# A factorization machine on one core: V's loads go first on two queues, and GpSimd holds back x until two thirds of V have landed

## The reference

```python
def reference(x, V, bias, g_bias):          # x: int32 512 x 6250, V: fp32 6250 x 64
    xf = x.astype(V.dtype)
    xv = xf @ V
    sum_sq = jnp.sum(xv * xv, axis=-1)
    sq_sum = xf @ jnp.sum(V * V, axis=-1)
    linear = g_bias + xf @ bias
    return linear + (0.5 * (sum_sq - sq_sum))[:, None]
```

## Time and profile before

| | us |
|---|---|
| median of 3 runs | 48.98 (48.85 to 49.02) |
| profiled execution | 49.03 |
| its span | 47.2 |
| busy: DVE | 30.5 (65%) |
| busy: PE | 22.0 (46%) |
| busy: POOL | 20.5 (43%) |
| busy: ACT | 13.7 (29%) |

### The profile page before, as it was taken

How to read it: one execution, slowest core, us unless ns; L and a number is a source line. 1 busy time by engine, 2 the same in 40 slices (tenths; PEclk the granted TensorE clock), 3 DMA queues, 4 the chain that set the end, 5 groups by cost and what they waited for, 6 DMA issues and landing times.

```text
span 47.2 us, 634 instructions
## 1 busy us (share of the span) xinstructions
PE 22.0 (46%) x210; PEld 20.1 (43%) x210; DVE 30.5 (65%) x74; ACT 13.7 (29%) x30; POOL 20.5 (43%) x34
## 2 busy tenths in 40 slices
PE   0000000000000000045999995999999999997200
PEld 0000000000000000045989893998999899985100
DVE  2000000000999469997999899999999999998600
ACT  0000009100899469954996300020002000000000
POOL 1999800000199009999599999990000000000000
PEclk9999999999999999999999999999999999999998
DMA  0399999999999999999999999999999970000000
GB/s 0 102 152 100 109 140 152 164 189 158 175 174 172 181 170 178 146 142 108 105 106 106 106 106 106 101 104 103 116 96 101 94 55 3 0 0 0 0 2 0
DMA packets 5583, 4.87 MB, mean 103 GB/s; under 512 B 1434, under 2 KB 5581, under 8 KB 5581
## 3 DMA queue, kind: packets, MB, share of 16 engines
q0 software_dynamic: 3456, 3.21, 73.4%
q1 hardware_dynamic: 1155, 0.82, 6.7%
q10 hardware_dynamic: 970, 0.81, 5.3%
HBM read 14.48 MB, written 0.00 MB: 307 GB/s over the span
## 4 chain that ended last, share of the span: by engine, by line
DVE 42%; DMA 34%; ACTq 10%; issue 4%; PE 2%; ACT 1%
DMA v_in<-in_L_rec_V_dram 34%; DVE x_all L330 13%; DVE seen L344 13%; ACTq L150 5%; DVE v_rest L295 3%; ACTq L237 3%; DVE xv L354 3%; DVE w_sum L301 2%; DVE xv_sq L359 2%; DVE odd_turned L335 2%; PE xv_ps L466 2%; ACTq L233 2%; DVE seen L406 1%; ACTq L234 1%; DVE seen L350 1%
## 5 line engine op out<-in xcount | busy, mean ns | idle before, releaser
L466 PE MATMUL xv_ps<-wall,x_all 128*128 128x195 bf16 x192 | 19.9, 266 | 1.8 <-DVE x_all L330 1.8
L466 PEld LDWEIGHTS xv_ps<-wall,x_all 128*128 128x128 fp8e4 x192 | 18.0, 105 | 2.7 <-DVE x_all L330 1.1
L160 POOL DMA_DIRECT2D x_all<-in_r_x_dram x24 | 13.0, 551 | 0.8 <-POOLq L498 0.8
L216 POOL TENSOR_TENSOR wall<-v_rest 128x512 bf16<-128x512 f32 (+1 forms) x6 | 7.4, 1247 | 10.2 <-DVE v_rest L295 10.2
L450 PE MATMUL g_ps<-g_in,ones 1*128 1x1 f32 x2 | 0.6, 342 | 20.2 <-DMA g_in<-in_L_rec_g_bias_dram 20.2
L450 PEld LDWEIGHTS g_ps<-g_in,ones 1*128 1x128 f32 x2 | 0.5, 305 | 20.2 <-issue 20.2
L330 DVE STREAM_TRANSPOSE x_all<-x_all 128x512 uint32<-128x512 uint32 (+1 forms) x13 | 8.5, 652 | 0.0
L364 DVE MEMSET v_in<- 22x64 f32 x1 | 0.1, 112 | 10.6 <-DMA v_in<-in_L_rec_V_dram 10.6
L344 DVE TENSOR_TENSOR seen<-seen,x_all 128x512 uint32<-128x512 uint32 (+1 forms) x10 | 6.3, 628 | 0.0
L251 ACT ACTIVATE v_sq<-v_in 128x512 f32<-128x512 f32 (+1 forms) x6 | 3.8, 636 | 5.3 <-DVE v_in L364 3.5
L295 DVE TENSOR_TENSOR v_rest<-v_in 128x512 f32<-128x512 f32 (+1 forms) x6 | 4.3, 750 | 1.4 <-DMA v_in<-in_L_rec_V_dram 1.3
(11 more groups left out here) (27 smaller groups left out, 9.5 us busy)
## 6 DMA issues: line engine op xcount, KB each, us to landing
x_all<-in_r_x_dram POOLq DMA_DIRECT2D x12, 196.0 KB, 9.7
v_in<-in_L_rec_V_dram ACTq DMA_DIRECT2D x6, 128.0 KB, 13.3
v_in<-in_L_rec_V_dram SPq DMA_DIRECT2D x6, 128.0 KB, 11.3
x_all<-in_r_x_dram POOLq DMA_DIRECT2D x4, 100.0 KB, 7.4
x_all<-in_r_x_dram POOLq DMA_DIRECT2D x4, 64.0 KB, 8.5
x_all<-in_r_x_dram POOLq DMA_DIRECT2D x4, 32.0 KB, 8.1
bias_in<-in_L_rec_bias_dram ACTq DMA_DIRECT2D x3, 6.5 KB
v_in<-in_L_rec_V_dram SPq DMA_DIRECT2D x1, 24.0 KB
```

The costliest lines, as they stand in the source:

```text
L160: queue.dma_start(x_words[S * i:S * i + S, t, :, lo // QUAD:hi // QUAD].bitcast(fp8), rows[:, :, START[i] + lo:START[i] + hi]).then_inc(x_ ...
L216: nc.gpsimd.tensor_tensor(placed(n, 2), v_part(v_rest, n), upper(v_rest, n), ALU.subtract).then_inc(low_placed, 1)
L466: last = nc.tensor.matmul(xv_ps[t][:, :, :], rows[:, q, :], wall[:, 1 + QUAD * d + q, :, 0:E], start=(d + q == 0), stop=(d == ND - 1 and q ...
```

## The change

POOL gets one wait ahead of its first x issue: `v_landed[1]` must be full, that is, V's second load must have landed in all four quarters. SP issues nothing but V's quarters 0 and 1 first; the odd rows of V go to ACT, behind its two DMAs of load 0; the five bias DMAs and g go behind V on SP. On DVE the two `sum_squares` of load 0 move ahead of the wait for the bias.

```diff
@@ block.sync
-            first = S * (NQ - 1)
-            sp.dma_start(v_in[0:first, 0, :],
-                         V[0:Q * (NQ - 1), :].rearrange("(i l) f -> i l f", l=Q)[:, 0:S, :]).then_inc(v_landed[0], 16)
-            sp.dma_start(v_in[first:P, 0, :], V[START[NQ - 1]:START[NQ - 1] + S, :]).then_inc(v_landed[0], 16)
             for n in range(NL):
                 load_v(sp, n, (0, 1))
+            sp.wait_ge(bias_cleared, 1)
+            sp.dma_start(bias_in[0:1, W - S:W], bias[0:S, :].rearrange("l o -> o l")).then_inc(bias_landed, 16)
...
+            sp.dma_start(g_in[:, :], g_bias.rearrange("(a b) -> a b", b=1)).then_inc(g_landed, 16)
@@ block.gpsimd
+            pool.wait_ge(v_landed[1], V_COUNT[1])
             load_x(pool, 0)
             load_x(pool, 1)
@@ block.scalar
+            first = S * (NQ - 1)
             load_v(act, 0, (2, 3))
-            act.wait_ge(bias_cleared, 1)
-            act.dma_start(bias_in[0:1, W - S:W], bias[0:S, :].rearrange("l o -> o l")).then_inc(bias_landed, 16)
...
+            act.dma_start(v_in[0:first, 0, :],
+                          V[0:Q * (NQ - 1), :].rearrange("(i l) f -> i l f", l=Q)[:, 0:S, :]).then_inc(v_landed[0], 16)
+            act.dma_start(v_in[first:P, 0, :], V[START[NQ - 1]:START[NQ - 1] + S, :]).then_inc(v_landed[0], 16)
             load_v(act, 1, (2, 3))
             load_v(act, 2, (2, 3))
-            act.dma_start(g_in[:, :], g_bias.rearrange("(a b) -> a b", b=1)).then_inc(g_landed, 16)
@@ block.vector
             keep_rest(0)
             keep_rest(1)
+            sum_squares(0)
+            sum_squares(1)
             dve.wait_ge(bias_landed, 16 * (NQ + 1))
...
-            sum_squares(0)
-            sum_squares(1)
             weigh(0)
```

More of the change, by code:

```diff
@@ L188, in _ @@
         def _(sp):
-            first = S * (NQ - 1)
-            sp.dma_start(v_in[0:first, 0, :],
-                         V[0:Q * (NQ - 1), :].rearrange("(i l) f -> i l f", l=Q)[:, 0:S, :]).then_inc(v_landed[0], 16)
-            sp.dma_start(v_in[first:P, 0, :], V[START[NQ - 1]:START[NQ - 1] + S, :]).then_inc(v_landed[0], 16)
             for n in range(NL):
                 load_v(sp, n, (0, 1))
+            sp.wait_ge(bias_cleared, 1)
+            sp.dma_start(bias_in[0:1, W - S:W], bias[0:S, :].rearrange("l o -> o l")).then_inc(bias_landed, 16)
+            sp.dma_start(bias_in[1:1 + ND, :], bias[S:Q, :].rearrange("(d l) o -> d (l o)", l=W)
+                         ).then_inc(bias_landed, 16)
+            for i in range(1, NQ):
+                sp.dma_start(bias_in[S * i:S * i + 1 + ND, :],
+                             bias[START[i] + S - W:START[i] + Q, :].rearrange("(d l) o -> d (l o)", l=W)
+                             ).then_inc(bias_landed, 16)
+            sp.dma_start(g_in[:, :], g_bias.rearrange("(a b) -> a b", b=1)).then_inc(g_landed, 16)
             y_out = out.rearrange("(p m) o -> p (m o)", m=T)
```

## The result

The changed kernel takes 54.11 us (53.41 to 55.03, 4 runs) against 49.0 us before: ratio 1.0992, 95% interval 1.0877 to 1.1107. It is 5 us slower where I had forecast 1.4 us faster. The profiled execution took 54.12 us with a span of 52.2.

What follows compares the result with a forecast made beforehand. The prediction took DVE's list and x's DMA stream, side by side, as the bound. DVE's slack of 0.54 us at tile 3 plus x landing 0.85 us earlier gave 1.4: 49.03 - 1.4 = 47.6 us, range 47.0 to 49.4.

Steps and rivals of the forecast that it cites:

- What bounds the kernel: DVE's work and x's DMA run side by side; DVE is only 1.25 and 0.54 us behind tiles 2 and 3.
- How fast V goes alone: V's loads on both queues without x: bounds 196 and 332 GB/s, 300 taken.
- When x starts: POOL's x loads after the wait: v_landed[1] full at 5.6 us, x's data flowing from 7.1 instead of 2.8.
- The gap is near nothing: DMA engines between V and x: V's last third ends at 7.1 us, when x's data begin to flow.
- When x lands: x's pieces 0 to 2 need 22.9 us at 105 GB/s; tile 2 lands at 30.3, 0.85 us earlier.
- The comparison: On the DMA engines: V costs x about 5.5 us when mixed in, 4.7 when put ahead.
- The bias: SP's bias loads behind V land at 9.5 us; DVE waits one microsecond, hidden by the wait for piece 0.
- POOL: POOL's eight x issues after the wait take 4.42 us, to 10.0; later pieces are issued without starvation.
- The sum: Whole kernel: 49.03 - 1.4 = 47.6 us, from 0.54 us of slack at tile 3 and x landing 0.85 earlier.
- Rival 1: V alone runs at the one-queue 196 GB/s: x flows from 9.0, end 1.1 us later at 50.1; chance 0.20.
- Rival 2: TensorE falls to its slow pace waiting for tile 2: 1.2 of 2.2 us count, 48.8 us; chance 0.12.

Runs made afterwards that it cites:

- e7: Kernel before with one 2048-column memset on POOL ahead of its first x issue; 48.93 us, ratio 0.9932 to the kernel before.
- e5: Changed kernel with V's odd rows behind all of ACT's V loads, POOL's wait kept; 51.24 us, ratio 1.0434 to the kernel before.
- e3: Changed kernel with POOL's wait on v_landed[0] in place of v_landed[1]; 52.81 us, ratio 1.0755 to the kernel before.
- e6: Changed kernel without POOL's wait and with V's odd rows back at the head of SP's queue; 57.4 us, ratio 1.1666 to the kernel before.
- e4: Changed kernel with 36 extra matmuls, read by nothing, behind tile 1's last one in TensorE's pause; ratio 1.0716 to the kernel before.
- e8: Kernel before with only V's odd rows moved from SP's head to ACT behind its load 0; 55.35 us, ratio 1.1174 to the kernel before.
- e2: Changed kernel without POOL's wait, the new queue order kept; 53.5 us, ratio 1.0851 to the kernel before.
- e1: Kernel before with only POOL's wait on v_landed[1] added, queues in their old order; 53.38 us, ratio 1.0756 to the kernel before.

## Why the prediction was wrong, point by point

- *What bounds the kernel* was read rightly. The slack of 1.25 us at tile 2 is what the short delays use up; in e7 DVE waits 2.12 us for tile 2 and loses nothing by it.
- *How fast V goes alone*: the step "Two queues at 196 each would be 392, so the engines cap them ... I take 300" held for V's own pieces: 292 GB/s, in the changed kernel for two microseconds and in e5 for all five. It failed for what stands between them. I had looked at the odd rows on SP as something that no longer stands in front, and not at the 128 pieces of 256 bytes that now stand in ACT's queue between its first loads and its second. With them the rate falls to 221 GB/s at a share of 0.99, and x's first issue comes at 10.19 instead of 7.11. The row of 196 GB/s was also read too simply: SP had issued the first 24 KB of odd rows by 1.7 us, so some of them may have been moving in it.
- *When x starts*: the step "5.3, and I add 0.3 ... 5.6" was mis-sized by 4.6 us. Of these 3.1 are the place of the odd rows (e5), and 1.5 remain even with V at 292 GB/s: 7.11 against 5.6. I had let the semaphore fill with the first 1.08 MB. Up to the end of the wait (9.89 in the changed kernel's chain; in e5 6.8, if the same 0.3 us lie between it and the first issue) the two kernels had moved:

```profile
1.00:9.89 8.89, 0.00 (x0) 0.00 (x0) 1.60 (x6) 2.84 (x5) 0.00 (x0) 1.00 0.76 183
```

```profile
1.00:6.80 5.80, 0.00 (x0) 0.00 (x0) 0.14 (x2) 1.42 (x2) 0.00 (x0) 1.00 0.91 249
```

These are 1.63 MB, all of V and the bias, and 1.44 MB, where loads 0 and 1 are 1.05. Load 2 thus moves beside load 1, and the wait "for two thirds" was in the changed kernel a wait for everything. "The gap is near nothing" was wrong with it: 2.2 us with a share of 0.04.
- *When x lands*: I had 1.5 + 0.3 + 22.9 = 24.7 us from issue to tile 2; measured 26.2, and 26.5 in e3 and e5. The start-up was right. By 36.4 us the engines had moved 57 times 1.8 and 106 times 23.4, 2.58 MB, 0.17 MB more than pieces 0 to 2 hold. So some engines were already in piece 3 while the last one finished piece 2: those 0.17 MB are 1.6 us at 106 GB/s. My sum had this term only for V (the 0.3 us) and at nothing for x.
- *The comparison* "V cost x about 5.5 us when mixed in ... It costs 4.7 when put ahead" is the step on which the sign hung. Put ahead, V costs 5.8 (e5) to 8.9 us, and what comes back is 3.7 in the changed kernel (29.9 - 26.2). The 5.5 was reckoned against an x that lands after 22.9 us at full rate. Of it 0.3 are x's slow start, and 0.8 the drift of the engines in the kernel before (0.09 MB at 106 GB/s); another 0.8 are lost because with x alone the drift is 1.6. As an estimate: 5.5 - 0.3 - 0.8 - 0.8 = 3.6.
- *The bias* was right in the changed kernel: DVE's `bias_in` memset at 11.22 follows the sums without a wait. e6 shows what the same place costs when x is not held back. *POOL* was right too: its eight issues took 4.42 us beside a busy DVE, as they had beside an idle one.
- *The sum*: at tile 2 I was 6.1 us off (36.41 against 30.3). By tile 2 alone my gain would have been 2.1, and I had taken 1.4 for tile 3's sake, so 0.7 of it are cover; TensorE adds 1.0. 6.1 - 0.7 + 1.0 = 6.4, and from -1.4 to +5.0 (the spans, 47.2 and 52.2) are 6.4.
- *The rivals.* Rival 1 (V slow, x from 9.0, end at 50.1) had the right mechanism and the right side, with x still 2 us too early. Rival 2 (slow matmuls, 1.2 us) came on top of it: it measured 1.0 by the traces and 1.35 by e4. I had 2.2 us for 32 slow matmuls (5.09 - 2.96 are 2.13); they took 1.6 more (4.55 against 2.96), the clock coming back before they were done. I had given each a chance and priced each alone; they are not independent, since the later x lands, the longer TensorE pauses. The Trainium skill's page "TensorE: Matmul & The Clock Gate", section "Part 1", names that fall of an idle array to 1.2 GHz, and the granted clock of 0.50 in the changed kernel's row agrees; e5's trace, with 1.00 after as long a pause, does not show it.

What stays open: why the engines drift apart by 1.6 us here and by 0.8 in the kernel before, and why the odd rows behind two loads on ACT delay `v_landed[0]` by as much as 5 us (e8). The Trainium skill's page "DMA: Bandwidth & Descriptors", section "Queues, rings and completion order", says that an engine takes its queues in turn, one packet of several descriptors from each. By that whatever stands in a queue behind other loads waits for a packet of x at every turn. The direction agrees with e2, e6 and e8; no run here shows a single turn, and why 32 KB cost so much is not answered by it.

## What to carry to other kernels

When one stream fills the DMA engines to the end, its later start is paid, and giving a smaller stream the engines for itself returns only what the two cost each other. Compare "time from first issue to landing" with and without the other stream before trading start for solitude, and count the small pieces in each queue, not its bytes. Ask also what else moves beside the loads that a semaphore stands for: here a wait for two thirds of V came to a wait for all of it. A short delay that lets the first few hundred KB and the small pieces of the other queues pass (here 0.35 to 1.2 us, ratios 0.985 and 0.993) can be worth a little where the consumer has slack; none of the four waits on a V semaphore tried here (changed kernel, e1, e3, e5) was. And where an engine will now wait for data, price its clock into the same case, not into another.

## What the hardware showed that I had not expected

- 36 useless matmuls made the kernel 1.35 us faster (e4), and the same pause of 3.5 us left the clock high in e5's trace and let it fall in the changed kernel's.
- Moving two DMAs of 32 KB in all from one queue's head to behind two loads on another cost 5.8 us (e8, ratio 1.1174).
- Beside a GpSimd that issues or computes, short DVE instructions stretch: `weigh(1)` of the changed kernel has 0.88, 0.95 and 1.01 us where 0.18 to 0.23 are usual. It is not the issues alone: `weigh(0)`, at 12.02 beside the eight issues, kept its 0.18. The end did not hang on it here.
